# One order for the whole program instead of one order for every turn

## The reference

```
x = x + 0.5 * ffn(layernorm(x))      # half 0
x = x + mamba(layernorm(x))          # scan
x = x + 0.5 * ffn(layernorm(x))      # half 1, the same weights

ffn(x):   x = x + attention(x)       # layernorm, 3-tap conv, qkv, rotary, 16 heads of 8, causal softmax, projection
          x = x + moe(x)             # layernorm, argmax router over 4 experts, gated 128 -> 512 -> 128
mamba(x): x = x + mamba2(x)          # 644 projections, 4-tap conv, silu, 4-head state scan, gated rmsnorm, projection
          x = x + mlp(rmsnorm(x))    # 128 -> 512 -> 128 with silu
```

## Time and profile before

| | us |
|---|---|
| median of 3 runs | 1969.23 (1958.37 to 1971.66) |
| profiled execution | 1961.06 |
| its span, first to last instruction | 1959.3 |
| PE busy | 1472.6 (75%) |
| DVE busy | 1202.9 (61%) |
| ACT busy | 808.2 (41%) |
| POOL busy | 386.4 (20%) |

### The profile page before, as it was taken

One profiled execution on the slowest core, in us unless ns is written; L12 is line 12 of the kernel. 1 busy time (PEld: TensorE's weight loads), 2 busy tenths in 40 slices (PEclk: granted clock), 3 DMA queues, 4 the chain that ended last, 5 costly groups with the idle time before them and its releaser, 6 DMA issues. The chain is left out here.

```text
span 1959.3 us, 30365 instructions
## 1 busy us (share of the span) xinstructions
PE 1472.6 (75%) x11328; PEld 779.5 (40%) x11328; DVE 1202.9 (61%) x2807; ACT 808.2 (41%) x1266; POOL 386.4 (20%) x396
## 2 busy tenths in 40 slices
PE   1366686578787898788978897879788987773855
PEld 0133343334343454444534453435344544332423
DVE  5344654476649675876678667867685648543532
ACT  0132243334353445444545454355545451441432
POOL 1001131031113211231223022402141214011111
PEclk9578598868788899899979897899888987886877
DMA  5203000202020303031301130032103100302101
GB/s 166 27 2 62 1 2 17 46 1 33 22 42 2 48 29 62 2 43 27 62 8 27 22 74 16 7 43 49 35 7 43 31 22 6 42 22 39 24 9 33
DMA packets 75807, 61.43 MB, mean 31 GB/s; under 512 B 6800, under 2 KB 71824, under 8 KB 75664
## 3 DMA queue, kind: packets, MB, share of 16 engines
q1 hardware_dynamic: 71568, 51.10, 14.8%
q0 software_dynamic: 4096, 8.40, 1.4%
HBM read 19.23 MB, written 14.55 MB: 17 GB/s over the span
## 5 line engine op out<-in xcount | busy, mean ns | idle before, releaser
L907 ACT ACTIVATE prob_mem<-aring 128x1024 f32<-128x1024 f32 x320 | 325.5, 1023 | 208.9 <-PE aring L639 203.3
L1266 DVE TENSOR_REDUCE mx<-aring 128x2 f32<-128x1024 f32 (+2 forms) x384 | 316.9, 861 | 138.3 <-PE aring L622 136.1
L597 PE MATMUL aring<-ramps,spots 64*128 64x128 bf16 (+1 forms) x2560 | 182.3, 223 | 137.1 <-DVE mx L1266 56.9
L729 PE MATMUL wring<-wv,scratch 128*128 x448 | 238.2, 646 | 6.8 <-ACT scratch L944 3.6
L597 PEld LDWEIGHTS aring<-ramps,spots 64*128 64x128 bf16 x2560 | 87.9, 99 | 339.8 <-issue 201.5
L582 PE MATMUL obank<-prob_mem,vx 128*9 128x512 f32 (+3 forms) x2048 | 199.7, 491 | 25.3 <-ACT prob_mem L907 15.0
L859 ACT ACTIVATE scratch<-wring 128x512 f32<-128x512 f32 x224 | 97.9, 437 | 179.7 <-PE wring L734 127.4
L1080 POOL DMA_INDIRECT got<-od,slot x64 | 63.3, 988 | 491.8 <-DMA od<-scratch 468.3
L1377 DVE SCALAR_TENSOR_TENSOR scratch<-scratch,wring 128x512 f32<-128x512 f32 x112 | 76.9, 686 | 135.0 <-ACT scratch L949 133.9
L639 PE MATMUL aring<-stq,stk 50*128 50x512 bf16 (+3 forms) x1024 | 141.5, 335 | 0.0
L622 PE MATMUL aring<-stk,stq 48*128 48x128 bf16 (+3 forms) x1024 | 137.0, 330 | 0.0
(11 more groups left out here) (211 smaller groups left out, 2429.2 us busy)
## 6 DMA issues: line engine op xcount, KB each, us to landing
hb<-hd SPq DMA_DIRECT2D x16, 448.0 KB, 3.5
stq<-high SPq DMA_DIRECT2D x96, 64.0 KB
stk<-high SPq DMA_DIRECT2D x96, 64.0 KB
stq<-mid SPq DMA_DIRECT2D x64, 64.0 KB
stk<-mid SPq DMA_DIRECT2D x64, 64.0 KB
od<-scratch SPq DMA_DIRECT2D x16, 256.0 KB, 3.0
od<-scratch SPq DMA_DIRECT2D x16, 192.0 KB, 2.1
x<-in_x SPq DMA_DIRECT2D x8, 256.0 KB, 2.8
```

The costliest lines, as they stand in the source:

```text
L597: pe.matmul(dst, spots[rows, 2 * by_key + part, :], ramp, start=(part == 0), stop=False, skip_group_check=True)
L729: last = pe.matmul(ring[:], hTd[:, u * P:(u + 1) * P], wv[:, expert[u], o:o + DFF], start=True, stop=True)
L907: act.activation(prob_mem[:, k], ring[:], ACT.Exp, scale=float(HD) ** -0.5).then_inc(freed, 1)
L1266: last = dve.tensor_reduce(mx[:, j, h0 + q:h0 + q + 3:2], ring[:, :, c:c + w], AX_X, ALU.max)
```

## The change

`ORDER` becomes a string of 1952 digits, one for each step of the program, and `plan` no longer starts afresh at each turn: every lane is one iterator over all turns. The sequence within each lane is the one of before (so the experts and the scans stay in one lane, in the same succession), and no buffer, bank count or instruction of a step is touched. Which bank a step gets follows the new order.

```diff
 ORDER = (
-    "11311121331233131321133311233133112302113113112331111331021033003310031131131501033331113110331031130311131311"
...
+    "00000000000000111111111111110110110111111111111001111111110101111111112212212022210111011111153013533333033333"
...
 )
 def plan(rows):
-    out = []
-    for i in range(-1, rows + LAG + 1):
-        lanes = [iter(lane) for lane in turn(i, rows)]
-        out += [(lane, *step) for lane in map(int, ORDER) if (step := next(lanes[lane])) is not None]
-        assert all(next(lane, None) is None for lane in lanes)
+    turns = [turn(i, rows) for i in range(-1, rows + LAG + 1)]
+    lanes = [iter([step for steps in turns for step in steps[lane] if step is not None]) for lane in range(len(turns[0]))]
+    out = [(lane, *next(lanes[lane])) for lane in map(int, ORDER)]
+    assert all(next(lane, None) is None for lane in lanes)
     return out
```

More of the change, by code:

```diff
@@ L157 @@
 ORDER = (
-    "11311121331233131321133311233133112302113113112331111331021033003310031131131501033331113110331031130311131311"
-    "13233113213231232131324332132151333313113333113130311401301313333013431033133313333331343333333141334131111111"
-    "411104311113311333333131"
+    "00000000000000111111111111110110110111111111111001111111110101111111112212212022210111011111153013333333033333"
+    "33133333333333311433131411111114111431131131133031331131313311131311331313323323323233333332121331231213331531"
@@ new lines @@
+    "31333113113031331333333333333333333333333103431130441110014131310013013333333311311313113331111331333100333133"
+    "31110301111112133123223120302321213113001153131331313113111310103113113131131311103113311113311333111331101313"
+    "11233113321134323113103323111410204110211431203121133011033335133111331131131133311333111133311003313113301113"
+    "11132132112231300323133201132311333113133131311333213113031133133111333110335311333310131133111313311341304101"
+    "33314331331314111313333121331321232333341123313211313123311344102110000111431310151330333331131313131113313311"
@@ new lines @@
+    "33133310130311103111311133123023321232301231323130231313331103113311333311333331103311311333013111333153113303"
+    "13114331103311113313133111433341113341111323313311233332331321331331131423111323111340141201201431131001133311"
+    "01333101333133135133311331133331103331110330111310132113213223103231302131132331133210311331313113331113331133"
+    "03113113331310130333311133113331141530313431133311133431411313111323133123123313113323311312331311233120334123"
+    "01404001510111431131133131133333331113113333113131333101003331113301113111321133211322300323133201132333311311"
@@ new lines @@
+    "03311333311333031123353113031133311313133331113330311133113311113343431133131413343101131311123311233123123113"
+    "33110331331131343112312040210140211413131113313013133331133311311313031313311331311331131531131131212131313131"
+    "12231131113122131113112331113313121333333333331133331131333153131311333101313311333341301314333331314323323334"
+    "23333333332333233024340024002043303333333333333331135313331313313133313131311311311133113113133113131311133130"
+    "11333331333310133111333113013113001110013103223233232332302211113511113141311331413333311333314131131413311311"
@@ L161 @@
+    "3331311331113113311131433113441111111124222222253333333333333333333333433333333444"
 )
 def plan(rows):
-    out = []
-    for i in range(-1, rows + LAG + 1):
-        lanes = [iter(lane) for lane in turn(i, rows)]
-        out += [(lane, *step) for lane in map(int, ORDER) if (step := next(lanes[lane])) is not None]
-        assert all(next(lane, None) is None for lane in lanes)
+    turns = [turn(i, rows) for i in range(-1, rows + LAG + 1)]
+    lanes = [iter([step for steps in turns for step in steps[lane] if step is not None]) for lane in range(len(turns[0]))]
```

## The result

| | before | after |
|---|---|---|
| median, us | 1963.8 (4 runs of this comparison) | 1796.55 (1787.46 to 1802.39, 4 runs) |
| ratio, 95% interval | | 0.9145 [0.9082, 0.9207] |
| profiled execution | 1961.06 | 1800.26 |
| its span | 1959.3 | 1798.4 |
| PE busy | 1472.6 (75%) | 1447.4 (80%) |

The change is worth 8.5%. The number of rival B, about 1800, was the nearest, though B is not what happened, as will be seen. And the miss of the sum is smaller than the misses in it, which in part cancel: the head was forecast too short, and the middle and the tail too long.

The account below looks back on a forecast made before the run. PE was near its limit only in the dense part, while core-less windows were one-stage chains. 71 + 312 + 1109 + 281 + 68 = 1841 us, 1843 with 1.8 around it, raised to 1847 toward the median; range 1800 to 1900.

Parts of the forecast that it names:

- rival B: Cores 1 and 2 absorb added work in 95 and 105 us, scan rounds gain 4 us each: about 1800 us; chance 0.10.
- the head: From the end of the start to core 3: 312 us where 419 stand, a gain of 107 us.
- the middle: Cores 3 to 13: 1109 us where 1124 stand, 15 us gained by covering shifts.
- the tail: From core 13's end through core 15: 72 + 102 + 27 + 80 = 281 us against 277.
- Rival A: Merged rounds not dense: cores 1 and 2 each 25 us more, dense part gains nothing; 1945 us, half 1895; chance 0.13.
- C: SP's queue delays shift DMAs in 23 more of 64 groups, 5.9 us each: about 1990 us; chance 0.04.
- D: New order changes little, idle windows being set by one instance's own chain: 1950 to 1980 us; chance 0.03.
- signs: Trace marks: core 1 near 133, core 3 near 383, cores 3 to 13 in 1090 to 1130 us, no long expert-load waits.
- 15 us for shift cover, and nothing for the other waits: Cores 3 to 13: 7 fewer uncovered shifts at 2.2 us make 15 us; other waits counted as no gain.
- the mean of the dense rounds: Cores 3 to 13 before the change, 1124 / 11 = 102 us, taken for core 1 and core 14.
- the right price of a covered shift: PE waited 2.2 us on average where under 1 us of PE work lay between last max and shift.

Follow-up runs that it names:

- the experiment on the head alone: First 342 steps of the new list, then the old order, against the kernel before: 1907.99 us, 0.9723.
- the new tail: Old order up to step 1675 (end of core 13), then the new succession, against the kernel before: 1918.51 us, 0.9775.
- The second list by hand: New list with core 2's first shift, fronts 14 and 15 earlier, eight core 14 steps among scan 7's first; against the kernel before: 1819.07 us, 0.9214.
- held stacks: New list, SP issuing all 24 stacking DMAs of fronts 5, 7, 9, 13 just ahead of the previous core's fourth shift; against the kernel before: 1791.92 us, 0.9112.
- the new middle alone: Old order with the new succession only from core 3's start to core 13's end, against the kernel before: 1932.65 us, 0.9842.
- both cures: New list with mid and low stacks of fronts 5, 7, 9, 13 issued behind the fourth shift; against the kernel before: 1790.36 us, 0.9072.

## Why the prediction was right and wrong

**Right: the direction, and the places.** Core 1 starts one us after core 0 (1.1), the gap of 81 us between them does not vanish but its work lies in core 1 (108 us, under the 125 that would have refuted it), core 3 starts at 406, and core 15 starts 24 us after core 14 (27 forecast). Not all signs held: core 3 was to start near 383, the clock is at its lower level for 92 of the 260 us between 130 and 390, the expert load of the end still ends a wait of 11.4 us (11.6 before), and one new wait for `stq<-shiftT`, 4.4 us, stands in core 0, behind front 1's stacks. Rival A (core 1 and core 2 each 25 us more, nothing gained behind) had half a point: together they take 26 us more than forecast, but the gaps shrank and the middle gained. Rivals C and D did not happen: the waits for the shift's DMA fell, from 35.4 us in 8 to 11.9 in 5 over the whole program, where C wanted 23 more, and the experiment on the head alone shows its gain.

**Wrong: "15 us for shift cover, and nothing for the other waits".** This step of the middle gave 1109 and 1077 came, 46 us under before instead of 15. The 15 came true as far as they went: PE's waits for the shift fell from 48.0 to 33.6 us. What failed is the "nothing" for the rest. The five waits of 29.6 us for the shift's DMA stood in the earlier trace rows and were counted only as something that might multiply. Their removal is worth 38 us in the old list (60 transfers moved, nothing else), and moving the same transfers in the new list brings no less idle time (137.8 against 134), so the new list had that gain already. The maxima gained 16 us of idle time too, which had been put at nothing, and others lost 17. The parts can't be added to 46 exactly, and no run separates them. Whether 2.2 us was the right price of a covered shift stays open as well: laying 43 of them bare costs 3.2 each, of which only 1.7 are the waits for the shift.

**Wrong: the tail at the mean of the dense rounds.** Core 14 was given 102 us, the mean of the dense rounds, but those hold 120 steps each (1318 in 11) and it has 103: 48 of its own, 27 of scan 7, 20 of experts 13, seven of front 15 and a load. At the prediction's own 0.853 us a step that is 88 us, and 89.6 came. PE is busy for 85 of them and waits for only 4.9. Twelve more steps beside core 15 were given 9 us and took none: PE was busy for 57.6 of 71 us there and is for 59.6 of 66.5 now. The gap before core 14 was given 72 us and took 65. Run alone, the new tail has 90.7 and 65.8 us for these two cores, so this does not hang on the rest.

**Wrong in the other direction: the head.** Core 2 was given 140 steps at 0.853 us. It takes 1.01 a step: PE is busy for 115.8 us, 0.83 a step against 0.72 in the dense part, since more of its steps are scan's and experts' and its clock is 0.80 on average; and it waits for 26 us, 7.4 of them before one shift. (The second list by hand moved a shift of core 2 earlier, and core 2 took 144 us instead of 141.) Core 0 was left at 60 and takes 70: PE's work rose from 40.0 to 46.1 us for 6 more instructions, at a clock of 0.65 instead of 0.74, and the stacking of front 1 now moves beside it (DMA share 0.19, before 0.01). Both excesses are read from windows; no run undoes either, so how much is the clock's and how much the mixture's stays open.

**Rival B** gave nearly the right time for the wrong places. It wanted cores 1 and 2 in 95 and 105 us and they took 108 and 142; its 20 us in the scan rounds were the real part, since the even cores from 4 to 12 take 34 us less than before in all. The rule of the Trainium skill cited there (Trainium Kernel Development and Optimization, Performance Expectations) asks for weight-load share instead of matmul share; the middle went from 0.447 to 0.455 in loads and from 0.844 to 0.876 in matmul, so there was room, as the prediction read it, and what bounded it was waits. Neither share told how much.

## What to carry to other kernels

When a list of steps is rearranged, take each wait of the densest stretch that is over some 5 us, ask what would take it away, and price that too, not only what could add more of its kind. Price a merged round by what meets there. Here 103 steps took 90 us, 140 took 141 and 88 took 66, and neither the mean of full rounds nor one rate per step gives all three; the sum of each engine's busy time in the pieces, and a look at which of them wait, is what I would try next, and no run here tests it. And small transfers that a matmul will wait for want distance in time from bulk transfers, wherever these stand in a queue; a trace shows such a case as a wait that ends where the DMA share falls to zero.

## What was not expected of the hardware

**A small transfer behind bulk lands late by whichever issuer.** Issued 0.05 us behind 12 stacking transfers with a 448 KB load ahead of them, the shift's pair let PE go on 11.7 us after its issue began; from ACT's queue such pairs still cost 32.7 us in 7 waits. Directly behind 24 stacks but with no load near, PE went on after 5.3 us (core 4 with held stacks), and with 4.4 us or more between them (cores 6, 8 and 12 there) it did not wait.

**One core's clock, 7 us.** Core 10 takes 106.6 us in the change, with the new middle alone and in the second of the lists by hand, and 98.7 to 99.7 in the other four kernels with the new middle's order that keep most shifts covered (one profiled execution of each). The window of core 10, in the change and then in the kernel with both cures:

```profile
1080.90:1187.50 106.60, 87.51 (x653) 43.54 (x652) 80.07 (x192) 46.71 (x72) 27.10 (x25) 0.79 0.16 30
```

```profile
1077.80:1177.50 99.70, 80.71 (x648) 42.49 (x642) 79.51 (x192) 46.62 (x72) 27.09 (x25) 0.85 0.19 34
```

PE's idle time is the same, 19.1 and 19.0 us; its busy time differs by 6.8 for the same work. Both fall to the lower level (0.50, 1.2 GHz) at the end of a stretch in which PE was busy for some 6 of 10 us, beside a front's DVE and POOL work, the first line of each three:

```profile
1110.90:1120.90 10.00, 6.13 (x57) 2.78 (x55) 5.46 (x8) 2.28 (x3) 7.07 (x8) 0.96 0.42 87
1120.90:1130.90 10.00, 5.83 (x41) 1.74 (x41) 8.15 (x21) 4.68 (x6) 1.64 (x3) 0.50 0.77 113
1130.90:1140.90 10.00, 9.31 (x42) 4.31 (x42) 3.71 (x12) 4.33 (x7) 2.83 (x4) 0.50 0.18 33
```

```profile
1107.90:1117.90 10.00, 5.81 (x56) 2.72 (x54) 5.84 (x9) 2.28 (x3) 7.76 (x8) 0.99 0.45 99
1117.90:1127.90 10.00, 5.96 (x48) 1.62 (x46) 7.45 (x19) 4.68 (x6) 0.94 (x1) 0.50 0.77 110
1127.90:1137.90 10.00, 9.31 (x55) 4.82 (x52) 6.18 (x18) 5.24 (x9) 3.51 (x6) 0.82 0.31 43
```

In the change the last 10 us shown are at 0.50 as well, in the other at 0.82. Why the clock returns sooner there isn't shown. A difference of some 0.4% between two orders can be this and nothing of their waits.
